# A two-layer kernel's recurrent cell: gate products as one 32-bit product each, in place of three products of high and low halves

## The reference, cut to what matters

```python
x = x + attn_ref(layernorm(x), W, b, input_bias, scale)   # the recurrent cell
x = x + ffn_ref(layernorm(x), ...)                        # attention, then experts

# inside attn_ref
pre = einsum('btd,df->btf', x, W) + b          # x: 128 features, W: 128 x 512
i_pre, f_pre, o_pre, z = split(pre, 4)         # four gates of 128 columns
i_gate = 10 * tanh((i_pre + input_bias) / 10)
f_gate = -softplus(f_pre)
o_sig  = sigmoid(o_pre)
tz     = tanh(z)
# then a scan over the 256 positions (running maximum, c, n, h), and an RMS norm
```

## Time and profile before

| | us |
|---|---|
| median of three runs | 1122.47 |
| the three runs | 1125.63, 1116.11, 1122.47 |
| span of the profiled execution | 1104.0 |
| cell and attention together | about 0 to 740 of the span |
| experts | about 760 to 1040 |
| last sum | 1046 to the end |

### The profile page before, as it was taken

The page is one execution under the profiler, slowest core; times in us unless marked ns, Lnnn a source line. Parts: engine busy times, 40 slices in busy tenths (PEclk is TensorE's granted clock), DMA queues, the critical chain, the costliest instruction groups (busy, mean ns, idle before and its releaser), DMA issues. The chain is left out here.

```text
span 1104.0 us, 26712 instructions
## 1 busy us (share of the span) xinstructions
PE 945.3 (86%) x7190; PEld 731.5 (66%) x7237; DVE 886.6 (80%) x2573; ACT 708.2 (64%) x1740; POOL 607.5 (55%) x797
## 2 busy tenths in 40 slices
PE   1467999999998998998999989950799999999574
PEld 1246677776775776776767766630799999999521
DVE  4568899999999999999999988576477777777368
ACT  2754888885885885885877646450466566566346
POOL 7211345445666766767858677586255565556400
PEclk9958999998999998999999999885799999999889
DMA  1024545353353353354343446142333332332096
GB/s 53 1 75 118 127 114 117 84 127 91 97 141 96 100 138 96 107 140 98 108 119 101 137 120 158 53 101 79 87 91 89 94 91 84 93 92 70 18 255 196
DMA packets 137975, 114.73 MB, mean 104 GB/s; under 512 B 19314, under 2 KB 126456, under 8 KB 137860
## 3 DMA queue, kind: packets, MB, share of 16 engines
q1 hardware_dynamic: 120772, 92.24, 32.4%
q0 software_dynamic: 8640, 16.93, 4.8%
q10 hardware_dynamic: 8448, 4.20, 1.3%
HBM read 60.60 MB, written 52.58 MB: 103 GB/s over the span
## 5 line engine op out<-in xcount | busy, mean ns | idle before, releaser
L595 POOL TENSOR_SCALAR_AFFINE_SELECT b_PT<-b_PT 128x256 f32<-128x256 f32 (+1 forms) x384 | 194.9, 525 | 179.2 <-ACT b_PT L776 175.4
L1125 DVE TENSOR_REDUCE b_m_neg<-b_ps_m 128x2 f32<-128x512 f32 (+1 forms) x384 | 257.5, 678 | 38.9 <-PE b_ps_m L1542 21.1
L776 ACT ACTIVATE b_PT<-b_ps_s 128x512 f32<-128x512 f32 x384 | 221.8, 601 | 42.6 <-PE b_ps_s L1518 21.7
L1874 POOL DMA_INDIRECT results<-e_Y,e_X x142 | 148.5, 1045 | 125.3 <-DVE e_Y L1941 102.4
L630 POOL DMA_INDIRECT slots<-c_pay,b_pos x128 | 129.9, 1015 | 36.9 <-issue 26.2
L1989 PE MATMUL e_ps_d<-e_h,e_w 128*128 128x256 f32 x568 | 135.0, 381 | 0.0
L1521 PE MATMUL b_ps_s<-c_QK 128*128 128x512 f32 x256 | 114.7, 450 | 8.9 <-ACT b_PT L776 8.9
L1542 PE MATMUL b_ps_m<-c_QK 128*128 128x256 f32 x512 | 119.9, 323 | 0.0
L1901 ACT ACTIVATE e_h<-e_ps,e_w 128x256 f32<-128x256 f32 x284 | 111.4, 480 | 0.8 <-PE e_ps L1980 0.8
L1989 PEld LDWEIGHTS e_ps_d<-e_h,e_w 128*128 128x128 f32 x568 | 103.0, 191 | 11.2
L1535 PE MATMUL b_ps_m<-c_QK 128*128 128x128 f32 x512 | 100.1, 320 | 7.9 <-DMA c_QK<-qk_scr 7.9
(11 more groups left out here) (242 smaller groups left out, 2418.7 us busy)
## 6 DMA issues: line engine op xcount, KB each, us to landing
c_QK<-qk_scr SPq DMA_DIRECT2D x128, 192.0 KB
qk_scr<-b_qk_hi SPq DMA_DIRECT2D x64, 256.0 KB, 2.5
e_X<-slots SPq DMA_DIRECT2D x71, 130.0 KB, 2.3
qk_scr<-b_qk_lo SPq DMA_DIRECT2D x32, 256.0 KB, 2.7
f_G<-results SPq DMA_DIRECT2D x32, 256.0 KB, 3.7
a_X<-in_L_attn_x_dram SPq DMA_DIRECT2D x16, 256.0 KB, 6.2
x<-a_X SPq DMA_DIRECT2D x16, 256.0 KB, 2.8
b_X<-x SPq DMA_DIRECT2D x32, 128.0 KB, 5.4
```

Source lines behind the costliest of these rows:

```text
L595: nc.gpsimd.affine_select(out=tri, in_=tri, compare_op=ALU.is_ge, fill=0.0, base=0, pattern=[[0, tri.shape[1]], [1, P]], channel_multiplie ...
L776: nc.scalar.activation(PT[:, g % 2, q % 3], ps_s[:, q % 2], ACT.Exp, scale=HD ** -0.5).then_inc(s_e, 1)
L1125: nc.vector.tensor_reduce(out, scores, AX.X, ALU.max, negate=True).then_inc(s_red, 1)
L1874: nc.gpsimd.indirect_dma_start(dram["results"][:, :], bass.IndirectOffsetOnAxis(X[:, j.of(NB_X), u, D:D + 1].bitcast(u32), 0), Y[:, n, u, ...
```

## The change

The weights stay as loaded, in one fp32 tile `cell.w`; the turned rows are copied once, without rounding, into one fp32 tile `cell.xt`. Each gate is one product of these two. The low half of the rows on DVE (`cell_low`), the halves of the weights (ACT at the start, DVE at the start) and the semaphores for them go. `cell_forget` and `cell_gate_i` wait for ACT's copy alone. The forget bias (L1453) stays as it was. No DMA is added or moved.

```diff
-        cell.w_hi = sb("a_w_hi", [P, 4 * D], f32r)
-        cell.w_lo = sb("a_w_lo", [P, 4 * D], f32r)
+        cell.w = sb("a_w", [P, 4 * D])
-        cell.xt_hi = sb("a_xt_hi", [P, 4 * P], f32r)
-        cell.xt_lo = sb("a_xt_lo", [P, 4 * P], f32r)
+        cell.xt = sb("a_xt", [P, 4 * P])
@@ ACT, at the start and in cell_high
-            nc.scalar.copy(cell.w_hi[:, :], cell_w_f[:, :]).then_inc(c_whi, 1)
-                nc.scalar.copy(cell.xt_hi[:, :], ps_r[:, :]).then_inc(c_xhi, 1)
+                nc.scalar.copy(cell.xt[:, :], ps_r[:, :]).then_inc(c_xc, 1)
@@ DVE
-            def cell_weights():
-                dve.wait_ge(c_whi, 1)
-                nc.vector.tensor_tensor(cell.w_lo[:, :], cell_w_f[:, :], cell.w_hi[:, :].bitcast(fp32), ALU.subtract).then_inc(c_prep, 1)
-            def cell_low(g):
-                if not g.exists(GROUPS):
-                    return
-                need(dve, c_xhi, g + 1)
-                need(dve, c_g, 4 * g)
-                nc.vector.tensor_tensor(cell.xt_lo[:, :], ps_r[:, :], cell.xt_hi[:, :].bitcast(fp32), ALU.subtract).then_inc(c_xlo, 1)
                     reduce(b1, 8)
-                    cell_low(gf)
                     reduce(b1, 9)
@@ PE
                 w = slice(c * D, (c + 1) * D)
-                nc.tensor.matmul(out, cell.w_lo[:, w], cell.xt_hi[:, :], start=(c != GF), stop=False)
-                nc.tensor.matmul(out, cell.w_hi[:, w], cell.xt_lo[:, :], start=False, stop=False)
-                nc.tensor.matmul(out, cell.w_hi[:, w], cell.xt_hi[:, :], start=False, stop=True).then_inc(c_g, 1)
+                nc.tensor.matmul(out, cell.w[:, w], cell.xt[:, :], start=(c != GF), stop=True).then_inc(c_g, 1)
             def cell_forget(g):
-                pe.wait_ge(c_prep, 13)
-                need(pe, c_xlo, g + 1)
+                need(pe, c_xc, g + 1)
             def cell_gate_i(g, c):
-                need(pe, c_xlo, g + 1)
+                need(pe, c_xc, g + 1)
```

More of the change, by code:

```diff
@@ L225, in sem @@
             return ctx.enter_context(nc.semaphore(name))
-        with nc.sbuf_tensor("a_w_f", [P, 4 * D], fp32) as cell_w_f, nc.sbuf_tensor("a_ones_f", [33, 512], fp32) as ones_rows, \
+        with nc.sbuf_tensor("a_ones_f", [33, 512], fp32) as ones_rows, \
                 nc.sbuf_tensor("b_w_f", [P, 3 * D], fp32) as w_f:
@@ L313, in layers @@
         c_prep = cell_sem("a_prep")
-        c_whi = cell_sem("a_whi")
         c_x = [cell_sem(f"a_x{k}") for k in range(NC)]
@@ L322, in layers @@
         c_xt = cell_sem("a_xt_s")
-        c_xhi = cell_sem("a_xhi")
-        c_xlo = cell_sem("a_xlo")
+        c_xc = cell_sem("a_xc")
         c_g = cell_sem("a_g")
@@ L464, in _ @@
             cell_rows(0)
-            sync.dma_start(cell_w_f[:, :], dram["W"]).then_inc(c_load, 16)
+            sync.dma_start(cell.w[:, :], dram["W"]).then_inc(c_load, 16)
             sync.dma_start(cell.b_col[:, :], dram["b"].rearrange("(c p) -> p c", p=P), allow_slow_non_contiguous=True).then_inc(c_load, 16)
@@ L961, in _ @@
             nc.vector.tensor_scalar(cell.bias_o[:, :], cell.b_col[:, GO:GO + 1], 0.5, None, ALU.mult).then_inc(c_prep, 1)
-            f_cols = cell_w_f[:, GF * D:(GF + 1) * D]
+            f_cols = cell.w[:, GF * D:(GF + 1) * D]
             nc.vector.tensor_scalar(f_cols, f_cols, 1.0 / CAP, None, ALU.mult).then_inc(c_prep, 1)
@@ L1414, in _ @@
                 step(Count(s))
-                if s == GROUND:
-                    cell_weights()
                 if s == -3:
```

## The result

| | before | changed |
|---|---|---|
| median of four runs | 1121.32 | 1135.83 |
| lowest and highest | 1116.11 to 1125.63 | 1128.26 to 1138.36 |
| ratio, 95% interval | | 1.0105 [1.0053, 1.0157] |

What follows compares the result with a forecast made beforehand. PE was taken as the chain from before the forget gate to `maximum(b1, 9)`, then DVE until PE's next wait. Loaded groups +7.7 and ramp -1.2 gave +6.5 us on 1122.5, so 1129.0, range 1117 to 1138.

Steps and rivals of the forecast that it cites:

- the case to which I gave 0.20: Whole kernel: slower by over 1%, a median above 1133.7 us, chance 0.20.
- PE is the chain: From before the forget gate to `maximum(b1, 9)`, PE sets the time; DVE's 0.60 us a group less gains nothing.
- Rival 1: Even step: DVE is the bound, so losing `cell_low` makes the kernel 8.4 us faster, 1114; chance 0.12.
- a stretch which repeats to 0.01 us: Forget bias to `cell_sums`, 15.65 and 15.64 us in two groups: taken as PE's full queue, not a neighbour's pace.
- The gate at 0.86 us: Each fp32 gate product takes 0.86 us, plus 0.13 opening on two gates: PE pays +0.71 us a group.
- Rival 2: Gates: fp32 products have opening costs before and behind each, +1.0 to +1.5 us a group, about 1137; chance 0.15.
- What comes back: Behind the z gate, PE's wait for ACT's second tanh is filled: -0.07 us, net +0.64 a group, +7.7 for twelve.
- The wait at `maximum(b1, 9)`: Head of the odd step: DVE's wait for PE grows from 0.96 to about 2.2 us.
- The ramp, -1.2 us: First four groups: forget gate's wait -0.73, slower-clock gate +0.43, net -0.3 each, -1.2 us in all.
- The start, "zero": Making the weights' halves goes; DVE's subtraction was hidden in its 1.30 us wait for `rstd`, so no gain.
- Rivals 3 and 4: 3: PE's growth is absorbed, 1122 within 2, chance 0.13; 4: the product runs in one pass, 1114 or less, 0.01.
- The stages behind: The experts and the last sum: taken not to change, any movement there left out.

Runs made afterwards that it cites:

- pe_part: From the changed kernel, a DVE pass of `cell_low`'s size put back, its result unused, with PE waiting for it: 1114.97 us, ratio 1.0088.
- dve_part: From the kernel before, `cell_low` removed and each gate's second product reading the high half instead, PE's work unchanged: 1102.82 us, ratio 0.9964.
- four_passes: The kernel before with a fourth `f32r` product in each gate (low halves of weights and rows), all else kept: 1133.77 us, ratio 1.0075.
- before_table: The kernel before with ACT's function table loaded at the very start of its queue: 1103.58 us, ratio 0.999.

## Why the prediction was right, and where not

The time and the range held: 1135.8 us against 1129.0, in 1117 to 1138. But I had forecast 0.6% more (6.5 of 1122.5 us), and the ratio, 1.0105, 1.0094 and 1.0106, is nearly twice that and lies on the border of the case to which I gave 0.20. The mechanism was right for what the change adds; one term was a little too large, another had the wrong sign, and they partly covered each other, which is luck.

- **PE is the chain, DVE's relief is worth nothing there.** Right for this change (pe_part, dve_part). Rival 1 and its 1114 fell. The rule of the Trainium skill (page "Perfetto Trace Analysis", section "Identifying the Most-Contended Engine"), by which DVE was the one to relieve, isn't borne out here: dve_part left the loaded stretch at 443.73 us. But my ground, that a stretch which repeats to 0.01 us isn't paced by a neighbour, was weak: with 0.91 us a group less on PE the stretch from bias to sums shrank by 0.17 only. In the strict sense PE wasn't the chain alone: less work on it brought nothing, since DVE's buffers and ACT's tanh stood right behind it. I had also passed over a row that pointed there, the waits of PE's weight loads for DVE, 13.3 us and 44 times in the kernel before, where I wrote that PE lost "a few us". The right side of it came out by the sign of the change, since load was added to PE and not taken away.
- **The gate at 0.86 us.** Right: 0.86 in the stream, 0.96 with an opening (I had 0.99), +0.65 and not +0.71 a group. The Trainium skill (page "FP8 and Floating Point Precision", section "TensorE Precision Notes") has four passes for true FP32; the trace agrees, 0.86 being four times 0.215. For the reduced type that section gives no number of passes; one was my reading, and the trace has one record, 0.227 us from start to start. Rival 2, opening costs everywhere, fell.
- **What comes back.** Sized at 0.07 a group, it measured 0.14 to 0.16 (score 1 and `values` besides score 0). Net 0.49 a group instead of 0.64: 11 groups gave +5.4 us, twelve +5.9 where I had +7.7. This is the mis-sized term.
- **The wait at `maximum(b1, 9)`.** Wrong as a sign: 0.80 and not 2.2 us. The extra idle time of DVE went to other reductions, 25.0 us and 33 times in all for 17.7 and 21.
- **The ramp, -1.2 us.** This step failed. The gates did come earlier (the fourth group's bias at 83.22 for 84.07), but the read-back behind the late landing set the end: from the first to the fifth bias +1.1 to +3.2 us over the 93.2 of before. four_passes, without the late landing, had +0.8. The clock isn't the cause: it was granted at 0.70 to 0.75 there in the traces with the fp32 gate and at 0.80 in the kernel before, but before_table, at 0.70 too, took only 92.14 us.
- **The start, "zero".** This step failed too. I named what hid DVE's subtraction, but not what ACT's removed copy did by the way: it drew a table load ahead of a wait. 1.35 us lost, 0.8 won by the missing hand-over to DVE (copy done to bias), +0.54.
- **Rivals 3 and 4.** Absorbed is a quarter (5.4 of 7.2 us came through), not all; and each gate is two records of 0.86 us together, not one pass.
- **The stages behind.** They don't change by the kernel, but they vary by chip and execution by more than the whole effect.

The sum from the traces: 5.9 + 0.5 + (1.1 to 3.2) = 7.5 to 9.6 us. The medians say 10.2 on chip A (1114.96 - 1104.81) and 9.8 on chip C (1114.9 - 1105.11) and 14.5 in the first comparison, whose interval reaches from 6 to 18. Some 0 to 3 us are unexplained.

## What to carry to other kernels

When two engines are both full, ask for each what a relief and what a load is worth; here PE's load counted at three quarters and more, PE's relief and DVE's relief alone at nothing, and only both together brought 4 us. And look in the relieved kernel for a wait that wasn't there before: PE's new wait for ACT's tanh showed that a third engine, busy for 64% of the span only, stood close behind. Before an instruction is removed, look at what it did besides its work: an early pass on ACT had its table loaded while nothing waited, and with it gone the load stood on the chain. And compare traces stretch by stretch between marks that both have, with a copy of each kernel on one chip, before any part of a difference between two spans is explained.

## What the hardware showed besides

- An fp32 product with 512 columns, divided by its four passes, costs a little less than an `f32r` product: 0.86 / 4 = 0.215 against 0.227 us.
- One table set served logarithm, exponential and identity: with it loaded at 3.43 us no further load came before the gates, where the kernel before made three loads of 1.28 us.
- Chips of the same kind ran the same program, the kernel before, at medians of 1104.8, 1105.1 and 1124.7 us. There is no trace of it from the third; the four traces of other kernels from that chip have 6 to 20 slots among the experts of 4.1 to 6.2 us instead of 3.59, those from the first two at most one.
- A write of 256 KB took 4.6 us to land in place of 2.8 in the five traces in which a packet of the instruction queue fell into it.
